# A two-layer megakernel on one core: how the convolution's input is loaded, and which queue carries VectorE's weight blocks

## What is computed

```python
x = x + conv(_layernorm(x))        # block-sparse causal convolution, 16 taps
x = x + ffn(_layernorm(x))         # 16 routed experts, top 6, and a shared expert
x = x + attention(_layernorm(x))   # 16 heads, 4 key/value heads, causal
x = x + ffn(_layernorm(x))

# conv: x (2, 512, 256) as 8 channel blocks of 64; 128 weight blocks (64, 64, 16 taps);
# block n reads channel block cols[n] and adds into channel block rows[n]
o = conv_general_dilated(x[:, cols], W, padding=[(ks - 1, 0)], feature_group_count=128)
y = zeros.at[:, rows].add(o)
```

## Time and profile before

| | us |
|---|---|
| median of 3 runs | 954.19 |
| the profiled execution | 955.55 |
| its span | 953.8 |
| first one-hot sum starts | 6.89 |
| convolve(0) starts | 59.08 |
| convolve(3) ends | 135.58 |

### The profile page before, as it was taken

The page is one execution under the profiler, slowest core; times in us unless marked ns, Lnnn a source line. Parts: engine busy times, 40 slices in busy tenths (PEclk is TensorE's granted clock), DMA queues, the critical chain, the costliest instruction groups (busy, mean ns, idle before and its releaser), DMA issues. The chain is left out here.

```text
span 953.8 us, 17012 instructions
## 1 busy us (share of the span) xinstructions
PE 925.5 (97%) x5729; PEld 807.3 (85%) x5729; DVE 545.4 (57%) x1378; ACT 439.1 (46%) x948; POOL 307.6 (32%) x268
## 2 busy tenths in 40 slices
PE   7999898999999999899999999999999999999998
PEld 6999786788888888568997897898887888888887
DVE  3679777633333333768768867866876533333333
ACT  6412142633433434357647656664662633343342
POOL 1310001145555555321212122121201255555553
PEclk8569799999999999999999999999999999999999
DMA  8489830111111110200100000000001111111111
GB/s 265 177 299 369 325 126 24 39 49 35 49 49 49 49 49 18 91 13 12 34 2 22 0 33 22 0 0 0 1 2 34 34 34 49 49 49 49 41 41 60
DMA packets 23537, 63.06 MB, mean 66 GB/s; under 512 B 3203, under 2 KB 11077, under 8 KB 20677
## 3 DMA queue, kind: packets, MB, share of 16 engines
q1 hardware_dynamic: 23492, 62.49, 19.5%
HBM read 61.43 MB, written 1.05 MB: 66 GB/s over the span
## 5 line engine op out<-in xcount | busy, mean ns | idle before, releaser
L834 DVE TENSOR_TENSOR f_h<-f_scaled,bank 128x512 f32<-128x512 f32 (+1 forms) x90 | 60.9, 676 | 183.5 <-POOL f_scaled L735 183.5
L735 POOL TENSOR_TENSOR f_scaled<-f_act,f_gate_rows 128x512 f32<-128x512 f32 (+1 forms) x90 | 113.4, 1261 | 135.7 <-ACT f_act L666 135.3
L924 PE MATMUL bank<-f_xt_hi,f_w_lo 128*128 128x512 f32 (+1 forms) x400 | 157.1, 393 | 0.0
L924 PE MATMUL bank<-f_xt_hi,f_w_hi 128*128 128x512 f32 (+1 forms) x400 | 156.6, 392 | 0.0
L673 ACT ACTIVATE f_h_hi<-f_h 128x512 fp32r<-128x512 f32 (+2 forms) x102 | 63.6, 624 | 183.6 <-DVE f_h L834 183.6
L924 PE MATMUL bank<-f_xt_lo,f_w_hi 128*128 128x512 f32 (+1 forms) x400 | 123.7, 390 | 0.1
L1103 ACT ACTIVATE at_prob<-bank,at_sbias,at_qrs 128x512 f32<-128x512 f32 (+3 forms) x128 | 77.6, 617 | 85.6 <-DVE at_sbias L1273 85.6
L941 PE MATMUL bank<-f_w_lo,f_h_hi 128*128 128x256 f32 (+1 forms) x400 | 113.2, 283 | 0.0
L941 PE MATMUL bank<-f_w_hi,f_h_lo 128*128 128x256 f32 (+1 forms) x400 | 113.1, 283 | 0.0
L941 PE MATMUL bank<-f_w_hi,f_h_hi 128*128 128x256 f32 (+1 forms) x400 | 113.1, 283 | 0.0
L843 DVE TENSOR_TENSOR f_h_lo<-f_h,f_h_hi 128x512 fp32r<-128x512 f32 (+2 forms) x102 | 70.2, 688 | 73.1 <-ACT f_h_hi L673 73.1
(11 more groups left out here) (185 smaller groups left out, 2000.3 us busy)
## 6 DMA issues: line engine op xcount, KB each, us to landing
cv_raw<-in_wconv SPq DMA_DIRECT2D x19, 1024.0 KB, 7.8
cv_shared<-in_wtaps SPq DMA_DIRECT2D x16, 768.0 KB, 7.2
f_wraw<-in_w SPq DMA_DIRECT2D x44, 256.0 KB, 2.7
f_wraw<-in_w SPq DMA_DIRECT2D x44, 128.0 KB, 2.5
at_wraw<-in_wqkv SPq DMA_DIRECT2D x3, 768.0 KB, 4.3
cv_shared<-in_x_blocks SPq DMA_DIRECT2D x4, 512.0 KB, 12.1
at_oraw<-in_wo SPq DMA_DIRECT2D x4, 512.0 KB, 3.6
cv_raw<-in_wconv SPq DMA_DIRECT2D x2, 512.0 KB, 4.6
```

The lines of the kernel that those rows point to most:

```text
L735: g.tensor_tensor(scaled[half][:, cols], act[half][:, cols], gate_rows[:, half * HALF + cols.start:half * HALF + cols.stop], ALU.mult).the ...
L834: v.tensor_tensor(h_f[half][0:rows, cols], src[half][0:rows, cols], pu[half][0:rows, cols], ALU.mult)\
L924: mm = t.matmul(bank[half][0:rows, :], w, x, start=q == 0, stop=q == len(steps) - 1)
```

## The change

The input is loaded once, as `x_tiles` into `X`, right after the third chunk; `x_blocks` is gone. The layernorm works on `X` in 8 tiles of 128x256 and writes the tile `xn`. The doubling and the shift between partition halves are done by the engines: ScalarE makes 8 instructions of 64x1024 into `xc_hi`, VectorE 8 into `xc_lo`, and GpSimd none. The 16 `wtaps` transfers are issued by GpSimd, one after another, when all of `xc_lo` is written; SyncE keeps the chunks.

```diff
+        def copies(b, k, par):
+            lo = KS - 1 - k
+            return (lambda x: x[k * BS:(k + 1) * BS, par::2, b, lo:lo + D],
+                    xn[par * BS:(par + 1) * BS, b * GC:(b + 1) * GC, :])
...
-            input_copies(0)
             blocks_first(2)
-            blocks_first(3)
-            input_copies(1)
-            for c in range(4, 8):
+            sp.dma_start(X[:].rearrange("p n t -> p (n t)"), ins["x_tiles"]).then_inc(s["x_in"], 16)
+            for c in range(3, NPE * (BS // CO)):
                 blocks_first(c)
-            taps_first(0)
-            blocks_first(8)
...
# ScalarE
-            round_banks(0, range(4, 6))
+            round_banks(0, range(4, 5))
             round_input(0, 0)
+            round_banks(0, range(5, 6))
+            round_input(0, 1)
             round_banks(0, range(6, 7))
-            round_input(0, 1)
+            round_input(1, 0)
             round_banks(0, range(7, 8))
...
             round_input(1, 1)
-            round_banks(1, range(2, 8))
+            round_banks(1)
# GpSimd
-            for b in range(B):
-                split_input(g, b, 1, s["xc_lo_g"])
+            g.wait_ge(s["xc_lo_done"], 4 * B)
+            for d in range(NDC):
+                if d >= 3:
+                    g.wait_ge(s["added"], 2 + 2 * DB * (d - 2))
+                g.dma_start(raw_d[d % 3], ins["wtaps"][d]...).then_inc(raw_d_in[d % 3], 16)
             following["powers"](g, 0)
# VectorE, the new order
+            low_banks(0, range(0, 2)); v.wait_ge(s["x_in"], 16); statistics(0); variances(0)
+            low_banks(0, range(2, 3)); statistics(1); variances(1); low_banks(0, range(3, 4)); (line_pair)
+            normalize(0); low_banks(0, range(4, 5)); normalize(1); low_banks(0, range(5, 7))
+            split_input(0, 0); low_banks(0, range(7, 8)); split_input(0, 1); low_banks(1, range(0, 1))
+            split_input(1, 0); low_banks(1, range(1, 2)); split_input(1, 1); low_banks(1, range(2, 5))
+            pairs = load_pairs(0); low_banks(1, range(5, 6)); add_blocks(0, pairs)
+            low_banks(1, range(6, 7)); low_banks(1, range(7, 8)); add_blocks(1, ...); add_blocks(2, ...)
```

More of the change, by code:

```diff
@@ L156, in conv_phase @@
         shared = sb("shared", [P, 3 * DB * DROW], F32)
-        x_dup = shared[:, 0:B * NCB * D].rearrange("p (b c t) -> p b c t", b=B, c=NCB)
+        xn = shared[:, 0:NT * D].rearrange("p (n t) -> p n t", n=NT)
         raw_d = [shared[:, i * DB * DROW:(i + 1) * DB * DROW].rearrange("p (n f) -> p n f", n=DB) for i in range(3)]
@@ L175, in conv_phase @@
         any_high = sb("any_high", [1, 1], I32)
-        stats, moments = sb("stats", [P, B * NCB, 6], F32), sb("moments", [P, B * NCB, 2], F32)
-        var_eps, rstd = sb("var_eps", [P, B * NCB], F32), sb("rstd", [P, B * NCB], F32)
+        stats, moments = sb("stats", [P, NT, 6], F32), sb("moments", [P, NT, 2], F32)
+        var_eps, rstd = sb("var_eps", [P, NT], F32), sb("rstd", [P, NT], F32)
         s = {n: cm(f"cv_{n}") for n in (
@@ L181, in conv_phase @@
             "count_ready", "flag_ready", "stats_done", "moments_done", "var_ready", "rstd_ready", "xn_ready",
-            "pads_ready", "xc_hi_done", "xc_lo_v", "xc_lo_g", "summed", "ws_hi_done", "ws_lo_done", "ws_free", "conv_done",
+            "pads_ready", "xc_hi_done", "xc_lo_done", "summed", "ws_hi_done", "ws_lo_done", "ws_free", "conv_done",
             "x_added")}
-        xd_in = [cm(f"cv_xd_in{b}") for b in range(B)]
         raw_in = [cm(f"cv_raw_in{i}") for i in range(3)]
@@ L207, in blocks_first @@
                 sp.dma_start(raw[c % 3][:], ins["wconv"][c]).then_inc(raw_in[c % 3], 16)
[L209 to L220, removed]
             sp.dma_start(colrow[:, 0:1], ins["cols"].rearrange("(n a) -> n a", a=1)).then_inc(s["cr_in"], 16)
@@ L255, in round_input @@
             def round_input(b, k):
[L256 to L260, removed]
+                if k == 0:
+                    a.wait_ge(s["pads_ready"], 2)
+                    a.wait_ge(s["xn_ready"], GC * (b + 1))
+                for par in range(2):
+                    dst, src = copies(b, k, par)
+                    a.activation(dst(xc_hi), src, ACT.Copy).then_inc(s["xc_hi_done"], 1)
             def round_banks(st, banks=range(SB)):
@@ L290, in _ @@
                 clear_sums(4 + q)
-            round_banks(0, range(4, 6))
+            round_banks(0, range(4, 5))
             round_input(0, 0)
+            round_banks(0, range(5, 6))
+            round_input(0, 1)
             round_banks(0, range(6, 7))
-            round_input(0, 1)
+            round_input(1, 0)
             round_banks(0, range(7, 8))
-            round_banks(1, range(0, 1))
-            round_input(1, 0)
-            round_banks(1, range(1, 2))
             round_input(1, 1)
-            round_banks(1, range(2, 8))
+            round_banks(1)
             for st in range(2, NPE):
@@ L304, in _ @@
                 round_sums(st)
[L306 to L312, removed]
         @block.gpsimd
@@ L330, in _ @@
             for b in range(B):
-                part = slice(b * NCB, (b + 1) * NCB)
+                part = slice(b * GC, (b + 1) * GC)
                 g.wait_ge(s["var_ready"], b + 1)
@@ L335, in _ @@
             g.wait_ge(s["rstd_ready"], B)
-            for b in range(B):
-                split_input(g, b, 1, s["xc_lo_g"])
-            g.wait_ge(s["xc_lo_v"], B)
-            g.wait_ge(s["xc_lo_g"], B)
+            g.wait_ge(s["xc_lo_done"], 4 * B)
+            for d in range(NDC):
+                if d >= 3:
+                    g.wait_ge(s["added"], 2 + 2 * DB * (d - 2))
+                g.dma_start(raw_d[d % 3], ins["wtaps"][d].rearrange("p (n f) -> p n f", n=DB)).then_inc(raw_d_in[d % 3], 16)
             following["powers"](g, 0)
@@ L393, in statistics, with split_input @@
             def statistics(b):
-                v.wait_ge(xd_in[b], 32)
-                for n in range(b * NCB, (b + 1) * NCB):
-                    v.bn_stats(stats[:, n, :], x_dup[:, b, n % NCB, :]).then_inc(s["stats_done"], 1)
+                for n in range(b * GC, (b + 1) * GC):
+                    v.bn_stats(stats[:, n, :], X[:, n, :]).then_inc(s["stats_done"], 1)
             def variances(b):
-                for n in range(b * NCB, (b + 1) * NCB):
+                for n in range(b * GC, (b + 1) * GC):
                     v.wait_ge(s["stats_done"], n + 1)
                     v.bn_aggr(moments[:, n, :], stats[:, n, :]).then_inc(s["moments_done"], 1)
[L402 to L405, removed]
+                v.wait_ge(s["moments_done"], (b + 1) * GC)
+                part = slice(b * GC, (b + 1) * GC)
+                v.tensor_scalar(var_eps[:, part], moments[:, part, 1], LN_EPS, None, ALU.add)                 .then_inc(s["var_ready"], 1)
             def normalize(b):
                 v.wait_ge(s["rstd_ready"], b + 1)
-                for c in range(NCB):
-                    n = b * NCB + c
-                    v.tensor_scalar(x_dup[:, b, c, :], x_dup[:, b, c, :], moments[:, n, 0:1], rstd[:, n:n + 1],
+                for n in range(b * GC, (b + 1) * GC):
+                    v.tensor_scalar(xn[:, n, :], X[:, n, :], moments[:, n, 0:1], rstd[:, n:n + 1],
                                     ALU.subtract, ALU.mult).then_inc(s["xn_ready"], 1)
+            def split_input(b, k):
+                for par in range(2):
+                    dst, src = copies(b, k, par)
+                    v.wait_ge(s["xc_hi_done"], 4 * b + 2 * k + par + 1)
+                    v.tensor_tensor(dst(xc_lo), src, dst(xc_hi).bitcast(F32), ALU.subtract).then_inc(s["xc_lo_done"], 1)
             low_banks(0, range(0, 2))
+            v.wait_ge(s["x_in"], 16)
             statistics(0)
             variances(0)
-            low_banks(0, range(2, 4))
+            low_banks(0, range(2, 3))
+            statistics(1)
+            variances(1)
+            low_banks(0, range(3, 4))
             v.wait_ge(s["line_in"], 32)
@@ L422, in _ @@
                                    op0=ALU.mult, op1=ALU.add).then_inc(s["cr_conv"], 1)
+            normalize(0)
             low_banks(0, range(4, 5))
-            normalize(0)
+            normalize(1)
             low_banks(0, range(5, 7))
-            statistics(1)
-            variances(1)
+            split_input(0, 0)
             low_banks(0, range(7, 8))
+            split_input(0, 1)
             low_banks(1, range(0, 1))
-            normalize(1)
+            split_input(1, 0)
             low_banks(1, range(1, 2))
[L432 to L435, removed]
+            split_input(1, 1)
+            low_banks(1, range(2, 5))
             v.sem_inc(s["added"], 2)
@@ L439, in _ @@
             pairs = load_pairs(0)
+            low_banks(1, range(5, 6))
+            add_blocks(0, pairs)
             low_banks(1, range(6, 7))
-            add_blocks(0, pairs)
-            pairs, more = load_pairs(1), load_pairs(2)
+            pairs = load_pairs(1)
             low_banks(1, range(7, 8))
```

(15 more changed lines are left out.)

1 line of the change is left out of this document (removed).

## The result

The changed kernel takes 949.22 us (median of 5 runs, 945.27 to 950.79) against 954.19 (5 runs, 953.85 to 955.92): ratio 0.9933, 95% interval [0.9905, 0.9961]. It is faster: by 5.0 us in the medians and 6.4 by the ratio, where 17 were forecast. One execution each of e10, of e11 and of the kernel before took far longer (3163, 1494 and 3127 us) and enters no ratio. The profiled execution took 945.27 us with a span of 943.5, the fastest of its times; a second trace, of the unchanged kernel run again (e1_again), has a span of 948.0, near the median. Both are needed.

A forecast was written before the change was run, and what follows sets the result against it. TensorE was taken as the bound, with its clock at half after waits for 1 MB chunks. Span 953.8 - 20.8 (earlier convolve(3) end) + 3.2 (late chunk, level VectorE) = 936.2, hence a forecast of 937 us, range 929 to 950.

The forecast's parts named there:

- the ledger: Kernel start: end times of statistics, splits and low banks by engine, with TensorE's bank 4 at 14.4 and bank 12 at 33.2 us.
- I take a fall about midway, at q12.: First sums: clock falls to half at bank 12, so banks 12 to 15 end at 46.9 us and convolve(0) at 54.5.
- TensorE has no DMA wait left at the start: First chunks: all land before TensorE wants them, chunk 3 at 17.8 us against 18.1, removing the 3.44 us wait.
- The row used as a bound: Kernel before, ahead of 18.10 us: clock fell within the first 1.3 us of TensorE's 3.44 us wait; a 0.3 us gap was harmless.
- I take one such delay, 2.2 us, and 1.0 for the level VectorE.: After convolve(0): one late chunk and VectorE running level with TensorE add 3.2 us in all.
- a delay of a block of over 2 us reaches the end: Steady part: VectorE's adds end at 113.2 us, just before TensorE's 114.8, so a later block would delay the end.
- GpSimd's issues at nothing: Sixteen block issues by GpSimd: taken as hidden at no cost, against an upper bound of 1.9 us each, 31 us.
- B: Rival: smaller gain, from slow half-partition splits, or from shared DMA making chunks late and the clock fall; 945 us, chance 0.17.
- A: Rival: clock holds to convolve(0), sums end 4.1 us sooner and convolve(0) saves 2.0; 931 us, chance 0.13.
- D: Rival: slower, blocks through GpSimd come late once landing exceeds 13.6 us; at 16 us each, 967 us; chance 0.11.
- The wide reading of the box: GpSimd's block issues: VectorE's two-port modes lock out descriptor writing, so each issue waits for VectorE; named as the last rival.
- The narrower statement: VectorE's adds: tensor_tensor has no two-port mode and takes only the read side, so adds don't stall GpSimd's issues.

The follow-up runs named there:

- e10: Changed kernel plus zero matmuls ahead of twelve banks where TensorE waits and block 0 loaded early, blocks in GpSimd's queue: 935.75 us, ratio 0.9807 to the kernel before.
- e11: Input part alone (blocks in SyncE's queue) plus sixteen transfers of 128 bytes issued by GpSimd: ratio 0.9944 to the kernel before.
- e1_again: The changed kernel unedited, run again for a second trace and five more times (also written e1): median 949.71 us, ratio 0.9951 to the kernel before.
- e12: Input part alone (blocks in SyncE's queue) plus one transfer of 128 rows of 3 KB issued by GpSimd: 946.23 us, ratio 0.9910 to the kernel before.
- e2: Input part alone: input loaded once, blocks issued by SyncE in the old order: 947.19 us, ratio 0.9928 to the kernel before.
- e5: Changed kernel plus zero matmuls of 512 columns ahead of banks 6 and 9 to 14, where TensorE waits: 945.87 us, ratio 0.9923 to the kernel before.
- e6: Changed kernel with one of the two add instructions of every block left out, computation incomplete: ratio 0.9884 to the kernel before.
- e3: Queue part alone: the kernel before with its 16 blocks issued by GpSimd and only chunks by SyncE: ratio 1.0015 to the kernel before.
- e4: Changed kernel plus two zero matmuls of 512 columns ahead of each of banks 8 to 15: 955.65 us, ratio 1.0021 to the kernel before.
- e7: Input part alone (blocks in SyncE's queue) plus one transfer of 512 bytes issued by GpSimd: 945.18 us, ratio 0.9915 to the kernel before.
- e8: Input part alone with chunk 15 put before block 10 in SyncE's order: ratio 0.9949 to the kernel before.
- e14: Changed kernel with block 0 loaded early and no added zero matmuls: ratio 0.9954 to the kernel before.
- e13: Changed kernel plus zero matmuls ahead of banks 6, 9 to 14, 20, 28, 30, 36 and 38, block 0 not early: ratio 0.9905 to the kernel before.

## Why the prediction was wrong

The bound was read rightly, and so was the first mechanism. The copies of the input were what held chunk 2; splits of 1.22 us, GpSimd's first issue at 40.4 (38.5 said) and the chain of low banks up to bank 10 came as in the ledger to within 2 us. The range held the median; the size was three times too large. By its own steps:

- **"I take a fall about midway, at q12."** The clock fell at bank 10 in one trace (c0 1.0 us later than the 54.5 said) and at chunk 3 in the other (5.6 us later). The ledger had chunk 3 there at 17.8, with 0.3 us to spare; it landed at 18.7. A miss of 0.3 to 0.7 us, which as a wait is nothing, decided over 4.6 us. So the statement "TensorE has no DMA wait left at the start" failed too. The row used as a bound (3.44 us of idleness) was far too long: single waits of 0.71 to 0.83 us (e12, e1, e2, e11) had the fall behind them. e5 shows the clock held when these short gaps are filled.
- **"I take one such delay, 2.2 us, and 1.0 for the level VectorE."** This term was mis-sized: from c0 to c3 60.3 + 3.2 = 63.5 us were forecast, 67.7 and 68.5 measured, so it is 7.4 and 8.2 us and not 3.2. The late chunk did not come. VectorE did fall behind, as the text said it might ("a delay of a block of over 2 us reaches the end"), with blocks 1.1 to 2.2 us late, and the price was left out: TensorE's wait for it, 1.0 to 1.4 us, brought the half clock, which costs more than the wait itself: in the changed kernel the sum from 83.88 takes 12.35 us instead of 7.3. e6, with half of the adds left out, takes 60.2 us without such a wait.
- **GpSimd's issues at nothing.** On VectorE that held: adds take 256 ns as before (255), and the blocks' median landing is 7.2 us, the chunks' 7.1. But 1.1 to 2.1 us come at the phase boundary, which the prediction carried over as it was: the 818.2 us behind convolve(3) are in its sum unchanged. e11 shows the longer wait, 1.3 us of this, to come from the number of transfers.

The three add up for the profiled execution to 1.0 + 4.2 + 2.1 = 7.3 us, its span (943.5) over the forecast (936.2), and for the second trace to 5.6 + 5.0 + 1.2 = 11.8 (948.0).

Of the rivals, B had the right mechanism for the second half (a small wait and the half clock) but laid it on the chunks. A was not what happened, though e10 shows that it can be had. D's threshold, a landing of 13.6 us, was not reached (the slowest block took 10.8). The wide reading of the box in the Trainium skill, SBUF — State Buffer ("DVE blocks DMA"), by which each issue waits for VectorE, would have shown blocks landing later than the chunks; in the trace they land alike, and an issue takes 0.54 us. The narrower statement there in the Trainium skill, under Who interferes with whom, agrees with the adds' 256 ns. A rule of the Trainium skill that bears on e3, in DMA: Bandwidth & Descriptors, Issuing engines are not separate DMA queues, says that a second issuing engine saves issue time and no bandwidth; e3's 1.0015 is in line with it.

What stays open: why sixteen transfers lengthen the boundary was not looked into, nor why chunk 3 lands 0.9 us later than worked out. What splits the times into groups is, by the traces, when TensorE starts its sums against chunk 3. In the unfilled kernels a start at 7.6 or 7.7 us gives a wait of 0.30 us or none and the fall at 27 us (changed, e6); a start at 6.2 to 7.4 us gives 0.71 to 1.44 us and the fall at about 19 (e1, e2, e4, e7, e8, e11, e12, e14; chunk 3 there at 18.7 to 19.0). This rests on one trace for each kernel, not on a trace of each execution.

## What to carry to other kernels

Where short matmuls run behind a wait, count what the wait does to the clock, not only its length: here a wait of 0.87 us cost 4.3 us up to the end of convolve(1) and one of 1.74 us cost 9 (e13 and e5 against e10's 20.9), and a wait removed moved the fall to the next one. Before valuing a change that shortens a stall, look for all smaller waits behind it, and fill them while the clock is still up (e5 against e4). Take a change apart: half of this one gave the whole gain, and the other half nothing that can be told and a longer wait in the next phase.

## What the runs showed of the hardware

- The one-hot sums hold full clock for 14.5 us, but don't win it back in 41 us; the 512-column matmuls of a convolve do, and two fills for each bank at half clock don't (e4, 0.50 over 33 us).
- Two short waits (0.69 and 0.87 us, in the profiled execution) are enough for a fall at 27 us, and one of 0.72 us for a fall at 19 us (e1); with fills, gaps of 0.22 to 0.25 us at the same places did no harm (e5, clock 1.00).
- A phase boundary costs TensorE 1.9 to 2.0 us without transfers from GpSimd or with one, and 3.2 to 3.3 with sixteen, of 768 KB as of 128 bytes.
